# Rows for the layer's far edge: copied between the layers into pieces of their own, instead of among the stores

## The chip, the cores and the metric

One core of one Trainium2 chip runs the whole program. The metric is the device time of one execution in microseconds. The kernel before takes 3490.39 us in the median of 3 runs (3487.72 to 3494.23).

## What is computed

The input x is (8, 16, 512, 512) in fp32: 8 images of 16 channels. Two layers, each adding something to its own input:

```python
x = x + fourier_conv(gn(x))       # layer 0
x = x + mean_filter_15x15(gn(x))  # layer 1
```

`gn` normalises groups of two channels over the whole image. Layer 0 takes the real 2-D FFT of the result, does a complex 3x3 convolution with 16 to 16 channels on the spectrum, adds a bias and transforms back. Layer 1 is a 15x15 box filter of each channel with zeros outside.

```python
kh = jnp.ones((1, 1, k, 1), x.dtype) / k
kw = jnp.ones((1, 1, 1, k), x.dtype) / k
y = lax.conv_general_dilated(xr, kh, (1, 1), [(pad, pad), (0, 0)])
y = lax.conv_general_dilated(y, kw, (1, 1), [(0, 0), (pad, pad)])
```

## The kernel before

One image lies in SBUF at a time, in `img` [128 partitions, T = 64 rows, W = 512]. A partition is one channel and one of HB = 8 blocks of 64 image rows; so step t of a loop over T works on row t of all 8 blocks of all 16 channels. The program loops over the 8 images. Images 0 to 6 run in a hardware loop in which the next image is loaded; image 7 runs after it and loads nothing.

Layer 0 works without an FFT: per row, matrices that are fetched from DRAM (`bd_all`), a Hilbert transform, and wave terms; TensorE, VectorE, ScalarE and GpSimd pass the row on (`gp`, `hp`, `g32`, `xT`, `kappa`, `bias_c`, `wrap_row`, `wrap_high` are its buffers). At its end come the statistics of the new x, which give the scale and shift of layer 1's norm.

Layer 1 keeps a running sum down the rows, in PSUM:

- GpSimd's `difference(u)` (L1479) makes row u + 7 minus row u - 8 of the image.
- ScalarE's `scale_row(u)` (L944, L945) scales it with the norm.
- TensorE's `turn_step(u)` (L757) transposes it, ScalarE's `high_part` (L810) and VectorE's `low_part` (L1332) split it into two fp16 parts.
- TensorE's `box_row(u)` (L768) adds the horizontal sum of these to the running row in `p0[0]`.
- VectorE's `add_box(u)` (L1340) adds x and writes the output row into `ob`, which has NS = 3 buffers of two rows. SyncE's `store` (L371) writes buffer j % 3 to DRAM with two DMAs of 256 KB. Before an even row u = 2j, `add_box` waits until the store of pair j - 3 has landed (`stored`).

The arena is cut into 16 pieces of one row each (`piece`, 512 fp32). In layer 1 `diff` is a ring of three pieces for differences (0, 1, 11), `parts` a ring of three for the fp16 parts (2, 3, 12); pieces 14 and 15 (`head`, `tail`) are presums.

Near a block's edges the box reaches into the neighbouring blocks, which lie on other partitions. For rows 1 to 7 `difference` needs the last 7 rows of the block before; for rows 57 to 63 the first 7 rows of the block after. DMAs from SBUF to SBUF bring them, both into the same pieces 4 to 10 (`across`):

- `rows_before` (L436) runs in the gap between the layers: zeros for the first block (`no_row`), then 4 copies of 4 rows, then 4 copies of 3 rows, as the rows become final (`x1_whole`). They signal `before_in`.
- `rows_after` (L451) runs in the loop of the stores, in two parts, because the pieces have to be read for the last time first (it waits for `turned`). Part 0 (rows 0 to 3) comes behind store pair 0, part 1 (rows 4 to 6) behind store pair 2; each is five DMAs, three of them with 32 partitions, one with 16, one of zeros from DRAM. They signal `after_in`.

Who waits for `after_in`: GpSimd before difference 57, and ScalarE's `load_next` (L964), because it overwrites the rows that were copied. `load_next` issues the loads of the next image from ScalarE's queue into rows that have been stored: at u = 11, 15, 19 and so on it loads 4 rows with two DMAs of 512 KB each, 8 rows behind.

The order on each queue is that of the program text. SyncE issues everything but the loads of images 1 to 7: in layer 0 the matrices and DMA transposes, then `rows_before`, then the 32 store pairs, with `rows_after` at j = 0 and 2 and a table (`hilbert_kernel`, 256 KB, into `tail`) at j = 4.

```python
for j in range(T // 2):
    ...
    store(b, j, j % NS)
    if j in (0, 2):
        rows_after(b, j // 2)
    if j == 4:
        sp.wait_ge(turned, b * T + 1)
        sp.dma_start(tail, tab["hilbert_kernel"]).then_inc(bias_in, 16)
```

Of the kernel before, what the change touches and what calls it, by code (L numbers as in the profile page):

```python
# [32 lines left out]
F16 = mybir.dt.float16  # L33
ALU = mybir.AluOpType
ACT = mybir.ActivationFunctionType
# [126 lines left out]
def build(nc, x, w_real, w_imag, b_real, b_imag, tab, bd_dram, out):  # L162
    x_v = x.rearrange("b c (s hl t) w -> b s c hl (t w)", s=2, hl=HL)
    out_v = out.rearrange("b c (s hl t) w -> b s c hl (t w)", s=2, hl=HL)
    with ExitStack() as ctx:
        def sb(name, shape, dt=F32):
            return ctx.enter_context(nc.sbuf_tensor(name, shape, dt))
# [18 lines left out]

        diff = [piece[s] for s in (0, 1, 11)]
        parts = [piece[s].bitcast(F16).rearrange("p (l k m) -> p l k m", l=2, k=NQ) for s in (2, 3, 12)]
        head, tail = piece[14], piece[15]
        across = [piece[4 + r] for r in range(R)]  # L190
        across_all = arena[:, 4 * W:(4 + R) * W]

        def diff_row(u):
            return across[u - 1] if u <= R else diff[u % 3] if u < T - R else across[u - (T - R)]

# [22 lines left out]
        xT = [row.bitcast(F16).rearrange("p (k m) -> p k m", k=8) for row in (piece[9], xT_more[:])]  # L218
        wrap_row = sb("wrap_row", [P, W], F16)
        wrap_high = sb("wrap_high", [P, W], F16)  # L220
        block_mat = sb("block_mat", [P, 9, P])
        kappa = sb("kappa", [P, 3, T, 2])
        bias_c = sb("bias_c", [P, 2, T, 2])
        known = sb("known", [P, T, 2])
# [63 lines left out]
        scaled_row = sem("scaled_row")  # L288
        before_in, after_in = [[sem(f"{name}{s}") for s in range(2)] for name in ("before_in", "after_in")]
        turned, high_done, low_done, banded = sem("turned"), sem("high_done"), sem("low_done"), sem("banded")  # L290
# [51 lines left out]
        def _(sp):  # L342
# [92 lines left out]

            def rows_before(b):  # L436

                def shifted(first, rows, signal):
                    to, at = across_all[:, first * W:(first + rows) * W], T - R + first
                    of = img[:, at:at + rows, :].rearrange("p t w -> p (t w)")  # L440
# [4 lines left out]
                sp.dma_start(across_all[0:HP:HL], tab["no_row"]).then_inc(before_in[0], 16)  # L445
                sp.wait_ge(x1_whole, (b + 1) * T - 3)
                shifted(0, 4, before_in[0])
                sp.wait_ge(x1_whole, (b + 1) * T)
                shifted(4, 3, before_in[1])

            def rows_after(b, part):  # L451

                first, rows = ((0, CHUNK), (CHUNK, R - CHUNK))[part]
                to = across_all[:, first * W:(first + rows) * W]
                of = img[:, first:first + rows, :].rearrange("p t w -> p (t w)")
                sp.wait_ge(turned, b * T + first + rows + 1)
                for hl in range(HL - 1):
                    sp.dma_start(to[hl:P:HL], of[hl + 1:P:HL]).then_inc(after_in[part], 16)
                sp.dma_start(to[HL - 1:HP:HL], of[HP:P:HL]).then_inc(after_in[part], 16)
                sp.dma_start(to[HP + HL - 1:P:HL], tab["no_row"][:, 0:rows * W]).then_inc(after_in[part], 16)  # L460

            with sp.Fori(0, B - 1) as b:
                matrices(b)
                rows_before(b)
                for j in range(T // 2):
                    if j == T // 2 - 2:
                        sp.wait_ge(loaded_pair[LAG // 2 - 1], b * 32 + 64)
                        sp.sem_inc(stores_held, 1)
                    store(b, j, j % NS)
                    if j in (0, 2):  # L470
                        rows_after(b, j // 2)
                    if j == 4:
                        sp.wait_ge(turned, b * T + 1)
                        sp.dma_start(tail, tab["hilbert_kernel"]).then_inc(bias_in, 16)
            matrices(B - 1)
            rows_before(B - 1)
            for j in range(T // 2):
                store(B - 1, j, j % NS)
                if j in (0, 2):
                    rows_after(B - 1, j // 2)  # L480
            for s in range(NS):
# [326 lines left out]
        def _(act):  # L808
# [35 lines left out]
            def image(b, follow):  # L844
# [67 lines left out]
                act.wait_ge(v_stacked, b + 1)  # L912
                nc.scalar.activation(wrap_high[:], p0[2], ACT.Identity, scale=sc[:, 27:28]).then_inc(v_high, 1)

# [82 lines left out]
        def _(dve):  # L997
# [193 lines left out]
            def layer0(b):  # L1191
# [27 lines left out]
                def low_hilbert(n, s):  # L1219
# [6 lines left out]
                dve.wait_ge(c_made, b + 1)  # L1226
                V.tensor_copy(bias_c[:], c_tab[:, 0:2])
# [4 lines left out]
                V.scalar_tensor_tensor(wrap_row[:], p0[2], sc[:, 26:27], wrap_high[:],  # L1232
                                       ALU.mult, ALU.subtract).then_inc(v_wrap, 1)
# [139 lines left out]
        def _(pool):  # L1373
# [89 lines left out]
            def layer1(b, follow):  # L1463

                def difference(u):

                    if u <= R:
                        pool.wait_ge(before_in[0], (b + 1) * 80)
                        if u > 4:
                            pool.wait_ge(before_in[1], (b + 1) * 64)  # L1470
                        more, less = img[:, u + R, :], diff_row(u)
                    elif u < T - R:
                        if u > R + 3:
                            pool.wait_ge(turned, b * T + u - 2)
# [47 lines left out]
```

## Time and profile before

| | |
|---|---|
| runs | 3494.23, 3487.72, 3490.39 us |
| the profiled execution | 3492.99 us |
| its span, first to last instruction | 3491.0 us |
| mean granted TensorE clock | 0.980 |
| TensorE busy | 3107.4 us (89%) |
| VectorE busy | 3076.4 us (88%) |
| GpSimd busy | 2723.9 us (78%) |
| ScalarE busy | 2446.0 us (70%) |

The profile is of one execution. Times in it are microseconds from the first instruction, those that are marked so are ns. PE is TensorE, DVE VectorE, ACT ScalarE, POOL GpSimd, SP SyncE; a q behind the name is the engine's sequencer, which issues DMAs. `<-` in brackets names what ended the idle time before an instruction. An image takes some 418 us (layer 1 begins at 465.82 in image 0 and at 883.76 in image 1), of which about 120 us are rows of layer 1. Seven images have the same course, the eighth loads nothing.

### The profile page before, as it was taken

To read this page: it belongs to the slowest core of one execution; us is meant where nothing else is said; L and a number is where in the kernel's file an instruction comes from. 1 tells how busy PE (TensorE), PEld (TensorE's weight loads), DVE (VectorE), ACT (ScalarE), POOL (GpSimd) and SP (SyncE) were. 2 spreads that over 40 slices of the span, in tenths; PEclk is the share of its full clock that TensorE was granted. 3 is DMA by queue.
4 is the path that set the end of the run, shared out by engine and by line. 5 is a ranking of instruction groups with operands and counts; after the bars stand their busy time and mean duration, and the time that the engine had idled before them with its cause. 6 is when DMAs were issued, how large, how long until landed. Compare 5 with 4: busy or idle time off the path is not lost.

```text
span 3491.0 us, 110788 instructions
## 1 busy us (share of the span) xinstructions
PE 3107.4 (89%) x36064; PEld 1869.7 (54%) x36064; DVE 3076.4 (88%) x5786; ACT 2446.0 (70%) x4742; POOL 2723.9 (78%) x2231
## 2 busy tenths in 40 slices
PE   2199979999889988899899998999988999899986
PEld 1155555555555555555555555555555555555555
DVE  6789978999889988899798997999978998889987
ACT  2568865787658876588666885578865787658876
POOL 4079975899749987599776997589974998759986
PEclk9699999999999999999999999999999999999999
DMA  8656668666876659766596666966678665876655
GB/s 206 200 93 128 127 202 252 114 127 120 249 205 126 128 116 285 169 125 128 154 293 125 126 129 184 272 113 128 120 225 229 117 128 119 259 195 126 127 129 174
DMA packets 726765, 573.58 MB, mean 164 GB/s; under 512 B 592416, under 2 KB 667776, under 8 KB 712064
## 3 DMA queue, kind: packets, MB, share of 16 engines
q1 hardware_dynamic: 704000, 451.67, 56.1%
q10 hardware_dynamic: 22400, 117.46, 13.1%
q8 instruction: 178, 2.92, 0.4%
q14 instruction: 187, 1.53, 0.2%
HBM read 262.08 MB, written 148.90 MB: 118 GB/s over the span
## 4 chain that ended last, share of the span: by engine, by line
PE 59%; DVE 16%; issue 9%; POOL 5%; DMA 3%; SPq 3%; ACT 1%; ACTq 1%; DVEq 0%; POOLq 0%
PE p L626 26%; PE h_ps L536 10%; PE h_odd L536 10%; DVE ob_all L1340 6%; DVE arena L1332 4%; PE p L633 4%; POOL arena L1479 3%; PE h_ps L626 3%; DMA out<-ob_all 2%; PE p L768 2%; DVE stat L1102 2%; PE h_ps L633 1%; PE p L575 1%; SPq L371 1%; ACTq L972 1%
## 5 line engine op out<-in xcount | busy, mean ns | idle before, releaser
L626 PE MATMUL p<-arena,bd_all 64*64 64x512 f16 x16896 | 1290.7, 381 | 31.2 <-DVE ob_all L1270 22.2
L626 PEld LDWEIGHTS p<-arena,bd_all 64*64 64x64 f16 x16896 | 555.2, 105 | 374.0 <-issue 233.1
L1419 POOL TENSOR_TENSOR ob_all<-ob_all,img 128x512 f32<-128x512 f32 x512 | 664.5, 1298 | 78.5 <-DVE ob_all L1264 52.2
L1422 POOL TENSOR_TENSOR ob_all<-ob_all 128x512 f32<-128x512 f32 x512 | 654.1, 1277 | 40.1
L1479 POOL TENSOR_TENSOR arena<-img 128x512 f32<-128x512 f32 x392 | 499.0, 1275 | 177.0 <-PE h_ps L757 97.9
L1264 DVE SCALAR_TENSOR_TENSOR ob_all<-p,bias_c,cosw 128x256 f32<-128x256 f32 x1024 | 447.6, 478 | 60.1 <-PE p L626 22.6
L886 ACT ACTIVATE img<-img,half_row (+1 forms) x1024 | 487.7, 528 | 5.0 <-ACT half_row L876 0.4
L768 PE MATMUL p<-band,arena 128*128 128x135 f16 (+1 forms) x4096 | 340.3, 228 | 154.9 <-DVE ob_all L1340 149.8
L1270 DVE SCALAR_TENSOR_TENSOR ob_all<-p,bias_c,cosw 128x256 f32<-128x256 f32 x1024 | 443.2, 474 | 0.0
L1412 POOL TENSOR_TENSOR arena<-arena 128x512 f16<-128x512 f32 x256 | 308.5, 1205 | 160.5 <-ACT arena L860 160.5
L859 ACT ACTIVATE arena<-img,sc 128x512 f16 (+1 forms) x512 | 433.8, 847 | 0.0
L944 ACT ACTIVATE arena<-arena,sc 128x512 f32<-128x512 f32 x392 | 282.9, 722 | 206.6 <-POOL arena L1479 197.9
L1340 DVE SCALAR_TENSOR_TENSOR ob_all<-p,img 128x512 f32<-128x512 f32 x512 | 347.5, 679 | 88.6 <-PE p L768 55.7
L1282 DVE BATCH_NORM_STATS2 stat<-img (+1 forms) x512 | 355.7, 695 | 51.7
L768 PEld LDWEIGHTS p<-band,arena 128*128 128x128 f16 x4096 | 260.5, 99 | 259.1 <-issue 244.6
L575 PE MATMUL p<-img,bd_all 128*64 128x256 f32 x2048 | 300.1, 402 | 92.6 <-POOL bd_all L1383 66.9
L536 PE MATMUL h_ps<-hilbert,arena 128*128 128x256 f16 x3072 | 379.8, 273 | 1.2 <-DMA arena<-arena 1.2
L536 PE MATMUL h_odd<-hilbert,xT_more 128*128 128x256 f16 x3072 | 379.8, 273 | 1.0 <-DMA xT_more<-arena 0.7
L1412 POOL TENSOR_TENSOR arena<-g_more,arena 128x512 f16<-128x512 f32 x256 | 311.7, 1218 | 55.5 <-ACT g_more L860 35.5
L536 PEld LDWEIGHTS h_odd<-hilbert,xT_more 128*128 128x128 f16 x3072 | 279.8, 98 | 138.2 <-issue 91.5
L536 PEld LDWEIGHTS h_ps<-hilbert,arena 128*128 128x128 f16 x3072 | 280.2, 98 | 132.6 <-issue 98.7
L1102 DVE BATCH_NORM_STATS2 stat<-img 128x6 f32<-128x512 f32 x512 | 334.8, 680 | 0.3
(182 smaller groups left out, 5136.6 us busy)
## 6 DMA issues: line engine op xcount, KB each, us to landing
out<-ob_all SPq DMA_DIRECT2D x512, 256.0 KB, 4.5
bd_all<-bd_dram SPq DMA_DIRECT2D x512, 224.0 KB, 2.5
img<-in_x ACTq DMA_DIRECT2D x168, 512.0 KB, 6.9
img<-in_x ACTq DMA_DIRECT2D x112, 256.0 KB, 5.3
img<-in_x SPq DMA_DIRECT2D x24, 512.0 KB, 26.1
arena<-img SPq DMA_DIRECT2D x48, 256.0 KB, 3.2
arena<-img SPq DMA_DIRECT2D x48, 192.0 KB, 2.7
bd_dram<-ob_all SPq DMA_DIRECT2D x11, 768.0 KB, 3.6
```

The costliest lines, as they stand in the source:

```text
L536: m = mm(dst(a), row[:, 4 * lx + k, :], tb["hilbert16"][:, lt, k, 0:cols], start=(half == 0 and i == 0), stop=(half == 1 and i == 2))
L626: m = mm(bank[out_half * HP:(out_half + 1) * HP, :], bd[s % RB][rows, 6 * lm + (j if own else j + 1), :], part, start=opens and i3 == 0, s ...
L768: m = mm(p0[0][:, lo:hi], parts[u % 3][:, l, k, :], tb["band16"][:, lo - k * P + R:hi - k * P + R], start=(u == 0 and k == 0 and l == 0), ...
L859: nc.scalar.activation(halves(gp[s][:, 0, :]), row, ACT.Identity, bias=sc[:, 9:10], scale=sc[:, 8:9])
L886: ins = nc.scalar.activation(row, row, ACT.Identity, bias=half_row[:, s, a:a + 1])
L1264: ins = V.scalar_tensor_tensor(t1[:, a, :], p1[:, a * HALF:(a + 1) * HALF], bias_c[:, 1, t, 1 - a:2 - a], cosw[:, a, :], ALU.subtract, ALU ...
L1270: ins = V.scalar_tensor_tensor(t2[:, a, :], p2[:, a * HALF:(a + 1) * HALF], bias_c[:, 0, t, 1 - a:2 - a], sinw[:, a, :], ALU.add, ALU.mult)
L1340: V.scalar_tensor_tensor(ob[j % NS][:, u % 2, :], p0[0], 1.0 / (K * K * BOX_SCALE), img[:, u, :], ALU.mult, ALU.add).then_inc(row_out, 1)
L1412: G.tensor_tensor(gp[s][:, 1, :], g32[s % 2], gp[s][:, 0, :], ALU.subtract).then_inc(g_split, 1)
L1419: G.tensor_tensor(q, term_row[s % 2][0], parity(img[:, t, :]), ALU.add).then_inc(first_added, 1)
L1422: G.tensor_tensor(q, q, term_row[s % 2][1], ALU.add).then_inc(q_done, 1)
L1479: G.tensor_tensor(diff_row(u), more, less, ALU.subtract).then_inc(moved, 1)
```

## The change

The rows of the block before go to pieces 0 to 6, those of the block after to pieces 7 to 13. They no longer share pieces, so the rows of the block after need not wait for a reader. All copies are issued in the gap between the layers (`rows_across`): the three DMAs of 32 partitions with 7 rows each stand between the two batches of rows of the block before, the DMA of 16 partitions and the one of zeros behind both. The store loop keeps the stores and the table. `rows_after` with its two parts is gone; `after_in` is one semaphore.

The rings that lay in these pieces go to buffers of layer 0 that layer 1 doesn't use: `diff` to `g32_more`, `xT_more` and the memory of `kappa` and `bias_c` (now one tensor, `biases`), `parts` to two stretches of `bd_all` and to `wrap_row` with `wrap_high` (now one tensor, `wrap_rows`). The rings keep three buffers.

```diff
-        diff = [piece[s] for s in (0, 1, 11)]
-        parts = [piece[s].bitcast(F16).rearrange("p (l k m) -> p l k m", l=2, k=NQ) for s in (2, 3, 12)]
         head, tail = piece[14], piece[15]
-        across = [piece[4 + r] for r in range(R)]
-        across_all = arena[:, 4 * W:(4 + R) * W]
+        rows_of_before, rows_of_after = arena[:, 0:R * W], arena[:, R * W:2 * R * W]
 
         def diff_row(u):
-            return across[u - 1] if u <= R else diff[u % 3] if u < T - R else across[u - (T - R)]
+            return piece[u - 1] if u <= R else diff[u % 3] if u < T - R else piece[R + u - (T - R)]
...
+        flat16 = bd_all[:].rearrange("p s r -> p (s r)")
+        diff = [g32_more[:], xT_more[:], biases[:, 0:W]]
+        parts = [row.rearrange("p (l k m) -> p l k m", l=2, k=NQ)
+                 for row in (flat16[:, 0:2 * W], flat16[:, 4 * W:6 * W], wrap_rows[:])]
...
                 sp.wait_ge(x1_whole, (b + 1) * T - 3)
                 shifted(0, 4, before_in[0])
+                to, of = rows_of_after, rows_of(0, R)
+                for hl in range(HL - 1):
+                    sp.dma_start(to[hl:P:HL], of[hl + 1:P:HL]).then_inc(after_in, 16)
                 sp.wait_ge(x1_whole, (b + 1) * T)
                 shifted(4, 3, before_in[1])
-
-            def rows_after(b, part):
-
-                first, rows = ((0, CHUNK), (CHUNK, R - CHUNK))[part]
-                to = across_all[:, first * W:(first + rows) * W]
-                of = img[:, first:first + rows, :].rearrange("p t w -> p (t w)")
-                sp.wait_ge(turned, b * T + first + rows + 1)
-                for hl in range(HL - 1):
-                    sp.dma_start(to[hl:P:HL], of[hl + 1:P:HL]).then_inc(after_in[part], 16)
-                sp.dma_start(to[HL - 1:HP:HL], of[HP:P:HL]).then_inc(after_in[part], 16)
-                sp.dma_start(to[HP + HL - 1:P:HL], tab["no_row"][:, 0:rows * W]).then_inc(after_in[part], 16)
+                sp.dma_start(to[HL - 1:HP:HL], of[HP:P:HL]).then_inc(after_in, 16)
+                sp.dma_start(to[HP + HL - 1:P:HL], tab["no_row"]).then_inc(after_in, 16)
...
                     store(b, j, j % NS)
-                    if j in (0, 2):
-                        rows_after(b, j // 2)
                     if j == 4:
                         sp.wait_ge(turned, b * T + 1)
                         sp.dma_start(tail, tab["hilbert_kernel"]).then_inc(bias_in, 16)
...
                     if t < R:
-                        act.wait_ge(after_in[t // CHUNK], (b + 1) * (16 * COPIES))
+                        act.wait_ge(after_in, (b + 1) * (16 * COPIES))
...
-                        pool.wait_ge(after_in[0 if u - (T - R) < CHUNK else 1], (b + 1) * (16 * COPIES))
+                        pool.wait_ge(after_in, (b + 1) * (16 * COPIES))
```

SyncE in the gap between the layers, before: a row is a line of the kernel, the destination and source of the DMA, partitions x elements, how many of them, and the semaphore that is waited for ahead of it; 2048 elements are 4 rows of the image, 1536 are 3, 3584 are 7.

```order
L445 DMA arena<-tab_no_row 16x3584 [waits p0_ready]
L442 DMA arena<-img 32x2048 [waits x1_whole]
L442 DMA arena<-img 32x2048 x2
L443 DMA arena<-img 16x2048
L442 DMA arena<-img 32x1536 [waits x1_whole]
L442 DMA arena<-img 32x1536 x2
L443 DMA arena<-img 16x1536
L371 ISA [waits row_out]
```

And now:

```order
L449 DMA arena<-tab_no_row 16x3584 [waits p0_ready]
L446 DMA arena<-img 32x2048 [waits x1_whole]
L446 DMA arena<-img 32x2048 x2
L447 DMA arena<-img 16x2048
L454 DMA arena<-img 32x3584 x3
L446 DMA arena<-img 32x1536 [waits x1_whole]
L446 DMA arena<-img 32x1536 x2
L447 DMA arena<-img 16x1536
L457 DMA arena<-img 16x3584
L458 DMA arena<-tab_no_row 16x3584
```

The three DMAs of L454 stand ahead of the wait for the last rows, two more behind the second batch.

SyncE at the stores around part 1 of `rows_after`, before: store pair 2 (four rows of L371, the first of which waits for the rows), the five copies, store pair 3.

```order
L371 ISA [waits row_out]
L371 DMA out<-ob_all 16x4x1024
L371 ISA
L371 DMA out<-ob_all 16x4x1024
L458 DMA arena<-img 32x1536 [waits turned]
L458 DMA arena<-img 32x1536 x2
L459 DMA arena<-img 16x1536
L460 DMA arena<-tab_no_row 16x1536
L371 ISA [waits row_out]
L371 DMA out<-ob_all 16x4x1024
L371 ISA
L371 DMA out<-ob_all 16x4x1024
```

And now, pairs 2 and 3:

```order
L373 ISA [waits row_out]
L373 DMA out<-ob_all 16x4x1024
L373 ISA
L373 DMA out<-ob_all 16x4x1024
L373 ISA [waits row_out]
L373 DMA out<-ob_all 16x4x1024
L373 ISA
L373 DMA out<-ob_all 16x4x1024
```

The copies are gone from between the pairs, and likewise those between pairs 0 and 1: each pair waits for its rows alone.

## Rows read from the trace of the kernel before

**Rows 1.** The page: the span; the group of add_box (columns: title of part 5).
```profile
span 3491.0 us, 110788 instructions
...
L1340 DVE SCALAR_TENSOR_TENSOR ob_all<-p,img 128x512 f32<-128x512 f32 x512 | 347.5, 679 | 88.6 <-PE p L768 55.7
```

**Rows 2.** Waits of the whole span (who <- whom: us in total, times, longest).
```profile
DVE ob_all L1340 <- PE p L768: 55.7, 168, 1.1
...
DVE ob_all L1340 <- DMA out<-ob_all: 32.7, 11, 4.9
```

**Rows 3.** Timeline, VectorE, image 0 (start us, us, ..., [idle <-releaser]).
```profile
465.82 0.68 DVE L1340 SCALAR_TENSOR_TENSOR ob_all<-p,img 128x512 f32<-128x512 f32 x1
...
482.92 0.69 DVE L1340 SCALAR_TENSOR_TENSOR ob_all<-p,img 128x512 f32<-128x512 f32 x1 [0.24 <-PE p L768]
...
489.07 0.69 DVE L1340 SCALAR_TENSOR_TENSOR ob_all<-p,img 128x512 f32<-128x512 f32 x1 [4.86 <-DMA out<-ob_all]
...
491.04 0.69 DVE L1340 SCALAR_TENSOR_TENSOR ob_all<-p,img 128x512 f32<-128x512 f32 x1 [0.68 <-PE p L768]
...
494.97 0.69 DVE L1340 SCALAR_TENSOR_TENSOR ob_all<-p,img 128x512 f32<-128x512 f32 x1 [0.24 <-PE p L768]
```

**Rows 4.** Timeline, VectorE, image 6, add_box of rows 0 and 15.
```profile
2972.67 0.68 DVE L1340 SCALAR_TENSOR_TENSOR ob_all<-p,img 128x512 f32<-128x512 f32 x1
...
3001.23 0.69 DVE L1340 SCALAR_TENSOR_TENSOR ob_all<-p,img 128x512 f32<-128x512 f32 x1 [0.67 <-PE p L768]
```

**Rows 5.** Timeline, VectorE, image 7 (no loads), rows 0 and 15.
```profile
3388.11 0.68 DVE L1340 SCALAR_TENSOR_TENSOR ob_all<-p,img 128x512 f32<-128x512 f32 x1
...
3411.44 0.69 DVE L1340 SCALAR_TENSOR_TENSOR ob_all<-p,img 128x512 f32<-128x512 f32 x1 [0.24 <-PE p L768]
```

**Rows 6.** Timeline, the queue of SyncE, image 0 (columns as in Rows 3).
```profile
449.21 0.59 SPq L443 DMA_DIRECT2D arena<-img  x1
453.97 1.74 SPq L442 DMA_DIRECT2D arena<-img  x3
...
473.09 2.87 SPq L371 DMA_DIRECT2D out<-ob_all  x4
476.00 2.49 SPq L458 DMA_DIRECT2D arena<-img  x3
...
479.17 0.59 SPq L460 DMA_DIRECT2D arena<-tab_no_row  x1
479.95 3.09 SPq L371 DMA_DIRECT2D out<-ob_all  x4
```

**Rows 7.** Timeline, the queue of ScalarE, image 0.
```profile
478.93 0.70 ACTq L972 DMA_DIRECT2D img<-in_x  x1
...
485.39 1.28 ACTq L972 DMA_DIRECT2D img<-in_x  x2
...
505.00 0.55 ACTq L972 DMA_DIRECT2D img<-in_x  x1
```

**Rows 8.** Chain of work, image 0 (start us, us, what).
```profile
480.75 8.30 DMA out<-ob_all
```

**Rows 9.** DMA issues at 477 to 478.9: KB each, median us to landing.
```profile
arena<-img SPq DMA_DIRECT2D x3, 192.0 KB, 3.0
```

**Rows 10.** DMA issues at 506.5 to 507.8, the same columns.
```profile
out<-ob_all SPq DMA_DIRECT2D x2, 256.0 KB, 6.6
```

**Rows 11.** Windows (line above the rows: columns), image 0.
```profile
core 0: us, PE busy (x) PEld busy (x) DVE busy (x) ACT busy (x) POOL busy (x), PEclk, DMA share, GB/s
...
470.00:481.00 11.00, 7.75 (x89) 6.28 (x87) 9.14 (x15) 7.95 (x14) 8.29 (x8) 1.00 0.92 299
481.00:485.00 4.00, 2.90 (x33) 2.24 (x30) 2.67 (x5) 3.30 (x7) 3.18 (x4) 1.00 1.03 240
486.00:489.00 3.00, 0.00 (x0) 0.00 (x0) 0.00 (x0) 0.72 (x1) 0.77 (x2) 0.54 1.03 404
...
500.00:560.00 60.00, 59.50 (x533) 36.91 (x532) 59.67 (x101) 39.87 (x67) 47.12 (x43) 1.00 0.99 288
```

**Rows 12.** DMA queues at 481.9 to 485.2: packets, MB, share of 16 engines.
```profile
q10 hardware_dynamic: 93, 0.62, 80.3%
q1 hardware_dynamic: 35, 0.11, 13.8%
```

**Rows 13.** DMA issues at 485.38 to 486.5 (columns as in Rows 9).
```profile
out<-ob_all SPq DMA_DIRECT2D x1, 256.0 KB, 10.6
```

**Rows 14.** Timeline, GpSimd, image 0, the first differences.
```profile
460.12 8.66 POOL L1479 TENSOR_TENSOR arena<-img,arena 128x512 f32<-128x512 f32 x7 [4.75 <-DVE arena L1345]
```

More of the change, by code:

```diff
@@ L218, in build @@
         xT = [row.bitcast(F16).rearrange("p (k m) -> p k m", k=8) for row in (piece[9], xT_more[:])]
-        wrap_row = sb("wrap_row", [P, W], F16)
-        wrap_high = sb("wrap_high", [P, W], F16)
+        wrap_rows = sb("wrap_rows", [P, 2 * W], F16)
+        wrap_row, wrap_high = wrap_rows[:, 0:W], wrap_rows[:, W:2 * W]
         block_mat = sb("block_mat", [P, 9, P])
-        kappa = sb("kappa", [P, 3, T, 2])
-        bias_c = sb("bias_c", [P, 2, T, 2])
+        biases = sb("biases", [P, 5 * 2 * T])
+        kappa = biases[:, 0:6 * T].rearrange("p (f t a) -> p f t a", f=3, a=2)
+        bias_c = biases[:, 6 * T:10 * T].rearrange("p (f t a) -> p f t a", f=2, a=2)
+        flat16 = bd_all[:].rearrange("p s r -> p (s r)")
+        diff = [g32_more[:], xT_more[:], biases[:, 0:W]]
+        parts = [row.rearrange("p (l k m) -> p l k m", l=2, k=NQ)
+                 for row in (flat16[:, 0:2 * W], flat16[:, 4 * W:6 * W], wrap_rows[:])]
         known = sb("known", [P, T, 2])
@@ L288, in build @@
         scaled_row = sem("scaled_row")
-        before_in, after_in = [[sem(f"{name}{s}") for s in range(2)] for name in ("before_in", "after_in")]
+        before_in, after_in = [sem(f"before_in{s}") for s in range(2)], sem("after_in")
         turned, high_done, low_done, banded = sem("turned"), sem("high_done"), sem("low_done"), sem("banded")
@@ L434, in matrices, with rows_across, rows_of @@
                 fetch(T - 1, (T - 1) % RB)
-            def rows_before(b):
+            def rows_across(b):
+                def rows_of(first, rows):
+                    return img[:, first:first + rows, :].rearrange("p t w -> p (t w)")
                 def shifted(first, rows, signal):
-                    to, at = across_all[:, first * W:(first + rows) * W], T - R + first
-                    of = img[:, at:at + rows, :].rearrange("p t w -> p (t w)")
+                    to, of = rows_of_before[:, first * W:(first + rows) * W], rows_of(T - R + first, rows)
                     for hl in range(HL - 1):
@@ L444, in rows_before @@
                 sp.wait_ge(p0_ready, (b + 1) * T + PRIMED)
-                sp.dma_start(across_all[0:HP:HL], tab["no_row"]).then_inc(before_in[0], 16)
+                sp.dma_start(rows_of_before[0:HP:HL], tab["no_row"]).then_inc(before_in[0], 16)
                 sp.wait_ge(x1_whole, (b + 1) * T - 3)
                 shifted(0, 4, before_in[0])
+                to, of = rows_of_after, rows_of(0, R)
+                for hl in range(HL - 1):
+                    sp.dma_start(to[hl:P:HL], of[hl + 1:P:HL]).then_inc(after_in, 16)
                 sp.wait_ge(x1_whole, (b + 1) * T)
                 shifted(4, 3, before_in[1])
-            def rows_after(b, part):
-                first, rows = ((0, CHUNK), (CHUNK, R - CHUNK))[part]
-                to = across_all[:, first * W:(first + rows) * W]
-                of = img[:, first:first + rows, :].rearrange("p t w -> p (t w)")
-                sp.wait_ge(turned, b * T + first + rows + 1)
-                for hl in range(HL - 1):
-                    sp.dma_start(to[hl:P:HL], of[hl + 1:P:HL]).then_inc(after_in[part], 16)
-                sp.dma_start(to[HL - 1:HP:HL], of[HP:P:HL]).then_inc(after_in[part], 16)
-                sp.dma_start(to[HP + HL - 1:P:HL], tab["no_row"][:, 0:rows * W]).then_inc(after_in[part], 16)
+                sp.dma_start(to[HL - 1:HP:HL], of[HP:P:HL]).then_inc(after_in, 16)
+                sp.dma_start(to[HP + HL - 1:P:HL], tab["no_row"]).then_inc(after_in, 16)
             with sp.Fori(0, B - 1) as b:
                 matrices(b)
-                rows_before(b)
+                rows_across(b)
                 for j in range(T // 2):
@@ L475, in _ @@
             matrices(B - 1)
-            rows_before(B - 1)
+            rows_across(B - 1)
             for j in range(T // 2):
                 store(B - 1, j, j % NS)
-                if j in (0, 2):
-                    rows_after(B - 1, j // 2)
             for s in range(NS):
@@ L912, in image @@
                 act.wait_ge(v_stacked, b + 1)
-                nc.scalar.activation(wrap_high[:], p0[2], ACT.Identity, scale=sc[:, 27:28]).then_inc(v_high, 1)
+                nc.scalar.activation(wrap_high, p0[2], ACT.Identity, scale=sc[:, 27:28]).then_inc(v_high, 1)
                 def slot(i, s, first):
@@ L1226, in layer0 @@
                 dve.wait_ge(c_made, b + 1)
-                V.tensor_copy(bias_c[:], c_tab[:, 0:2])
+                V.tensor_copy(bias_c, c_tab[:, 0:2])
                 lk(V.scalar_tensor_tensor(known[:], c_tab[:, 2], unscale, parity_mean, ALU.mult, ALU.add))
@@ L1231, in layer0 @@
                 dve.wait_ge(v_high, b + 1)
-                V.scalar_tensor_tensor(wrap_row[:], p0[2], sc[:, 26:27], wrap_high[:],
+                V.scalar_tensor_tensor(wrap_row, p0[2], sc[:, 26:27], wrap_high,
                                        ALU.mult, ALU.subtract).then_inc(v_wrap, 1)
```

## The prediction, as it stood before the change was run

> **What bounds the kernel now.** The page comes first, for the size of things: a span of 3491.0 us in an execution of 3492.99 us, and `add_box` (L1340), VectorE's last step of every row of layer 1 [rows 1]. The waits of the whole span say what this step waits for. Most of it is TensorE in small pieces of at most 1.1 us; but 32.7 us are eleven waits for a store of `ob_all` to land, the longest 4.9 us [rows 2]. Few and long: that is one place, not a rate.
>
> The timeline of VectorE shows the place. In image 0 `add_box` of row 0 starts at 465.82 and that of row 11 at 482.92, one row each 1.55 us. Row 12 starts at 489.07 after 4.86 us idle, "<-DMA out<-ob_all"; rows 13 and 15 still have 0.68 and 0.24 us of TensorE before them, and row 15 starts at 494.97 [rows 3]. So row 15 is 29.15 us behind row 0. In image 6 it is 28.56 us [rows 4]; in image 7, where no next image is loaded, 23.33 us [rows 5]. The disturbed images lose 5.8 and 5.2 us against the last one: I take **5.5 us in each of 7 images**, 38.7 us in all. (4.7 us of it is the wait itself, 32.7 / 7; the rest is TensorE coming back.)
>
> Why does row 12 wait? Store pair j takes rows 2j and 2j+1 out of one of three `ob` buffers, so row 12 needs pair 3 (rows 6 and 7) landed. Row 7 was ready at 477.4 (row 11's start less four periods, plus 0.69). But SyncE's queue shows L458, L459 and L460 from 476.00 to 479.76, the five copies of `rows_after` part 1, and pair 3 only behind them, at 479.95 [rows 6]. Meanwhile ScalarE's queue issued the first two loads of the next image, 512 KB each, at 478.93 and 479.79 [rows 7]. So the copies pushed the pair from 1.5 us ahead of the loads to 1.0 us behind them. Its second half, issued at 480.75, took 8.30 us and ended the wait at 489.05 [rows 8].
>
> **The change part by part.**
> *Removed.* SyncE issues ten copies fewer among the stores of each image. Part 0 sat where the queue had slack: nothing waits for pairs 0 to 2, I price it at nothing. Without part 1, pair 3 is issued at 477.4 and 478.2. Copies issued at 477 to 478.9, just as far ahead of the loads, landed in 3.0 us [rows 9]: the pair lands at about 481.5, and row 12 is due at 484.5. The wait at row 12 goes, with what follows it: at most −5.5 us an image.
>
> *What is late next.* Pair 4 (rows 8, 9) is ready at 480.5, and its second half is issued at 481.3, 1.6 us behind a load's issue. The nearest pair in that position (506.55, load at 505.00 [rows 7]) took 6.6 us in the median [rows 10]: landed at 488, row 14 is due at 487.6. I price it at 0 to 0.5 us, inside the next figure.
> Pair 5 (rows 10, 11) is ready at 483.6, behind the 256 KB copy of `hilbert_kernel` that stays where it was (j == 4). Row 16 is due at 491.0. The next two loads were issued at 485.39 [rows 7], a place that TensorE and ScalarE set before row 12's wait, so it stays. What must the 16 DMA engines move by then? Loads alone moved at 240 GB/s (481 to 485), stores after them at 404 GB/s (486 to 489), both with the engines full [rows 11]. From 481.0: two loads (1.05 MB) 4.4 us, pair 4 1.3 us, the table 1.1 us at the rate of a load, pair 5 1.3 us: 489.1, about 490 with the landing. But the second two loads join 2 us after their issue, at 487.4, with 1.7 us of this left. How are the engines shared then? At 481.9 to 485.2, with pairs waiting, ScalarE's queue (q10) held 80.3% of them and SyncE's (q1) 13.8% [rows 12]. With a fifth for the stores the pair lands at about 494.5 and row 16 waits 3.5 us; with half, at 491.8 and it waits 0.8 us. The worst pair of this stretch took 10.6 us from 485.29 [rows 13]; from 484.4 that would be 495.0, a wait of 4.0 us. The best case is none. I take 2.2 us, midway between the two shares, and 0.3 us for TensorE after it: **+2.5 us**.
>
> The Trainium skill (DMA: Bandwidth & Descriptors, Queues, rings and completion order) states that each engine goes round robin between the queue rows that have work, packet by packet. By that rule the wait at row 16 would be the 0.8 us of equal shares or less, and the sum 33 us or more, as in the second rival. This case's trace doesn't show equal turns: 13.8% against 80.3% in the stretch above [rows 12], so I keep the middle.
>
> *Added in the gap.* SyncE issues three copies of 448 KB (7 rows, 32 partitions) between the two batches of rows from the block before, and two of 224 KB behind. Issuing costs 0.6 us each, 449.85 to 451.8, and SyncE waits until 453.97 anyway [rows 6], so the second batch (L442, then L443) isn't issued later. But its 0.67 MB is behind 1.34 MB more. At the 299 GB/s of mixed copies and stores [rows 11] the three take 4.5 us from 452.6 and the batch 2.2 us more: landed at 460.3 instead of 458. Its first reader is GpSimd's difference of row 5. The first difference starts at 460.12, seven take 8.66 us [rows 14]: the fifth starts at 465.1. The cover is 4.8 us; if it were gone, every us of delay would be one on GpSimd, ahead of ScalarE and TensorE. Price: nothing. The last two copies are wanted by ScalarE's first load, 18 us later: nothing.
>
> *Moved rings.* `diff` and `parts` lie elsewhere, with three buffers as before, the same waits and the same instructions. No engine gets a longer operand. ScalarE's and GpSimd's waits on `after_in` become one wait that is long over. Nothing.
>
> *Behind row 16.* From 500 to 560 VectorE is busy 59.67 of 60 us, so rows come at its own pace, but the DMA engines are at 0.99 too [rows 11]. Copies of 1.8 MB leave this stretch, so a shift of rows 16 to 63 is kept; image 7 has no wait and gains nothing.
>
> **Sum:** (5.5 − 2.5) × 7 = 21 us off 3492.99, 3472 us. The profiled execution is 2.6 us above the median of the runs (3490.39), so I predict **3469 us**. 0.2%, some 7 us, is about what a measurement of this kernel can tell from no change.
>
> **The rivals.**
> 1. *Forecast: the wait shrinks and moves to row 16*, 0.8 to 3.5 us: 12 to 33 us off (the upper wait with 0.3 us of TensorE, the lower with none), 3457 to 3478. For it: the shares of 80.3% and 13.8% [rows 12]. Chance 0.55.
> 2. *It is gone:* pair 5 gets enough of the engines, because pair 3 and the last copies no longer queue in the way of the first loads: 38.7 us off, 3452. For it: the sum of work ends at 490, a microsecond before it is due. Against it: the table ahead of the pair. Chance 0.28.
> 3. *The change doesn't do what it says:* the loads, not the copies, hold up the stores, and the waits at rows 12 to 16 add up to what was there: 3490. For it: the 10.6 us of a pair with no copy ahead of it. Chance 0.11.
> 4. *The DMA engines become the bound, slower:* the wait at row 12 was a pause in which they caught up. Without it rows 16 to 56 carry a backlog, with store packets and load packets mixed all the time. Four rows are 2.1 MB; at the 288 GB/s of 500 to 560 they take 7.3 us, while VectorE needs 7.1 (101 instructions in 60 us, three a row [rows 11]). At 264 GB/s, midway to the 240 of loads alone, they take 7.95: 0.8 us on each of ten groups, 8 against the 5.5 us saved, 2.5 × 7 = 18 us more, 3508. It decides below 274 GB/s, where ten groups lose 5.5 us. Against it: the bytes from row 16 on are the same as before, and they fitted. Chance 0.06.
>
> **Range.** The full gain less a margin of 2 us gives 3450. The worst single pair (4.0 us, and 0.8 us of TensorE, whose granted clock was 0.54 at 486 to 489 [rows 11], near its lower level of 1.2 GHz, after it had stood idle in the wait) leaves 0.7 us × 7 = 5 us, 3485; the two shares end at 3478. I set the upper end at 3484, which leaves out rivals 3 and 4, 0.17. Faster: 0.83, the first two; same: 0.11; slower: 0.06.
>
> **What would show it.** Right: no "<-DMA out<-ob_all" before row 12 in images 0 to 6; pair 3 issued at once when row 7 is ready, landing in 3 to 4 us; a wait of about 2 us before row 16, its pair's second half landing close to the second loads; the copies of L454 and the batch behind them landed before GpSimd's fifth difference; image 7 unchanged. Wrong: a wait before row 5 of the differences; a wait that stays at row 12 with pair 3 issued early; waits at rows 14 or 30 and later that weren't there; or rows 16 to 56 slower than 1.8 us each, which would say that the DMA engines are the bound.

## The result, and the profile after

| | before | changed |
|---|---|---|
| median of the runs | 3490.39 us (5 runs, 3487.72 to 3494.23) | 3470.51 us (5 runs, 3466.16 to 3473.83) |
| ratio | | 0.9938, 95% interval 0.9926 to 0.9949 |
| the profiled execution | 3492.99 us | 3473.83 us |

Faster by 0.62%, 19.9 us by the medians, 19.2 us between the two profiled executions. The range of the prediction holds it, and the time is 1.5 us off the predicted one.

The page of the changed kernel: the span, and `add_box`, which is L1334 now [rows 1].

```profile
span 3471.8 us, 110748 instructions
...
L1334 DVE SCALAR_TENSOR_TENSOR ob_all<-p,img 128x512 f32<-128x512 f32 x512 | 348.2, 680 | 65.9 <-PE p L762 48.0
```

Waits of the whole span (who <- whom: us in total, times, longest), against [rows 2]:

```profile
DVE ob_all L1334 <- PE p L762: 48.0, 171, 1.2
...
DVE ob_all L1334 <- DMA out<-ob_all: 17.5, 20, 1.8
```

32.7 us in eleven waits have become 17.5 us in twenty, the longest 1.8 us. The waits are fewer microseconds, and they are spread.

The timeline of VectorE in image 0, rows 0, 11, 12, 14, 15, 16 and 18 of `add_box` [rows 3]:

```profile
466.87 0.68 DVE L1334 SCALAR_TENSOR_TENSOR ob_all<-p,img 128x512 f32<-128x512 f32 x1
...
483.97 0.69 DVE L1334 SCALAR_TENSOR_TENSOR ob_all<-p,img 128x512 f32<-128x512 f32 x1 [0.23 <-PE p L762]
...
485.57 0.69 DVE L1334 SCALAR_TENSOR_TENSOR ob_all<-p,img 128x512 f32<-128x512 f32 x1 [0.31 <-PE p L762]
...
489.71 0.69 DVE L1334 SCALAR_TENSOR_TENSOR ob_all<-p,img 128x512 f32<-128x512 f32 x1 [1.33 <-DMA out<-ob_all]
...
491.23 0.69 DVE L1334 SCALAR_TENSOR_TENSOR ob_all<-p,img 128x512 f32<-128x512 f32 x1 [0.23 <-PE p L762]
...
493.04 0.67 DVE L1334 SCALAR_TENSOR_TENSOR ob_all<-p,img 128x512 f32<-128x512 f32 x1
...
496.97 0.69 DVE L1334 SCALAR_TENSOR_TENSOR ob_all<-p,img 128x512 f32<-128x512 f32 x1 [0.27 <-DMA out<-ob_all]
```

Row 12 follows row 11 by 1.60 us, without a wait for a store. Row 14 waits 1.33 us, row 18 0.27 us. Row 15 stands 24.36 us behind row 0, where it stood 29.15.

The timeline of SyncE's queue in image 0 [rows 6]:

```profile
450.89 2.79 SPq L454 DMA_DIRECT2D arena<-img  x3
455.02 1.74 SPq L446 DMA_DIRECT2D arena<-img  x3
456.80 0.59 SPq L447 DMA_DIRECT2D arena<-img  x1
457.44 0.59 SPq L457 DMA_DIRECT2D arena<-img  x1
458.07 0.59 SPq L458 DMA_DIRECT2D arena<-tab_no_row  x1
469.26 13.72 SPq L373 DMA_DIRECT2D out<-ob_all  x10
483.09 0.60 SPq L470 DMA_DIRECT2D arena<-tab_hilbert_kernel  x1
484.83 4.39 SPq L373 DMA_DIRECT2D out<-ob_all  x4
```

The timeline of ScalarE's queue there [rows 7]:

```profile
479.99 0.69 ACTq L966 DMA_DIRECT2D img<-in_x  x1
...
486.45 1.55 ACTq L966 DMA_DIRECT2D img<-in_x  x2
```

The stores from 469.26 on are one run of ten DMAs, five pairs. DMA issues in three windows, 478.5 to 479.9, 481.5 to 482.9 and 484.5 to 486 (KB each, median us to landing), which are pairs 3, 4 and 5:

```profile
out<-ob_all SPq DMA_DIRECT2D x2, 256.0 KB, 3.0
...
out<-ob_all SPq DMA_DIRECT2D x2, 256.0 KB, 6.8
...
out<-ob_all SPq DMA_DIRECT2D x2, 256.0 KB, 6.2
```

Pair 3 is issued ahead of the loads (479.99) and lands in 3.0 us, pair 4 behind them in 6.8 us, pair 5 in 6.2 us. In the gap, the instructions of line L446 from 454.5 to 457, the second batch:

```profile
DMA to landing us min/median/max: 2.4/2.5/2.5
```

And the timeline of GpSimd's first differences [rows 14]:

```profile
461.17 8.66 POOL L1473 TENSOR_TENSOR arena<-img,arena 128x512 f32<-128x512 f32 x7 [4.76 <-DVE arena L1339]
```

No idle time inside the seven differences: the batch in the gap (issued by 457.4, landed in 2.5 us) was there 6 us before the fifth began at 466.1.

The table below says where the time went. Each number is the start of `add_box` of that row behind row 0 of its image, from the timeline, in the mean of images 0 to 6. The experiments that follow stand in the same table. "Stores" is the total of "DVE ob_all <- DMA out<-ob_all" in the waits.

| kernel | row 12 | row 14 | row 16 | row 24 | row 56 | row 63 | stores, us | median, us |
|---|---|---|---|---|---|---|---|---|
| before | 22.83 | 27.21 | 30.80 | 45.11 | 102.76 | 118.58 | 32.7 | 3490.39 |
| changed | 18.69 | 22.68 | 26.43 | 41.33 | 99.37 | 115.60 | 17.5 | 3470.51 |
| e1 copies back among the stores | 22.75 | 27.06 | 30.53 | 44.87 | 102.55 | 118.32 | 32.3 | 3491.18 |
| e2 small copies, load held too | 19.73 | 23.96 | 27.51 | 42.35 | 100.00 | 115.88 | 12.6 | 3470.07 |
| e3 before, without part 1 | 18.69 | 22.90 | 27.33 | 42.67 | 100.95 | 116.65 | 22.7 | 3463.47 |
| e4 table behind pair 0 | 18.69 | 22.67 | 26.00 | 40.85 | 98.67 | 114.66 | 13.1 | 3461.36 |
| e5 small copies, load not held | 21.87 | 26.10 | 29.53 | 43.84 | 101.83 | 117.75 | 27.1 | 3487.54 |
| e6 loads one row later | 18.79 | 23.23 | 26.82 | 41.62 | 98.98 | 115.16 | 11.9 | 3471.19 |
| e7 four store buffers | 18.69 | 21.81 | 25.15 | 39.45 | 96.97 | 112.71 | none | 3457.05 |
| e8 before, four buffers | 18.69 | 22.81 | 26.27 | 40.78 | 98.28 | 114.24 | 10.1 | 3464.82 |
| e9 four buffers, table first | 18.69 | 21.81 | 25.14 | 39.44 | 96.95 | 112.97 | none | 3452.99 |
| e10 before, part 1 behind pair 3 | 18.69 | 25.57 | 30.22 | 45.19 | 102.90 | 118.71 | 30.6 | 3494.76 |

The change saves 4.1 us an image at row 12, 4.4 at row 16, 3.8 at row 24, 3.4 at row 56 and 3.0 at row 63. 3.0 × 7 is 20.9 us (unrounded), the whole result of 19 to 20 us: row 0 of image 0 stands 1.05 us later in this execution (466.87 against 465.82), which takes the rest back. Image 7 stays at 98.13 us for row 63, as before. The rows are those of one execution of each kernel, the medians those of all its runs.

### The profile page after: what moved, and what is told of

The parts are those of the page before. It is cut to its first block, busy times and chain, and to the rows that moved or that the text cites. A ratio compares the mean times of both kernels' runs of the same rounds, so it can differ in the third digit from the quotient of the medians.

```text
span 3471.8 us, 110748 instructions
## 1 busy us (share of the span) xinstructions
PE 3104.5 (89%) x36064; PEld 1865.1 (54%) x36064; DVE 3079.8 (89%) x5786; ACT 2444.9 (70%) x4742; POOL 2726.1 (79%) x2231
## 3 DMA queue, kind: packets, MB, share of 16 engines
q10 hardware_dynamic: 22400, 117.46, 13.1%
## 4 chain that ended last, share of the span: by engine, by line
PE 61%; DVE 13%; issue 11%; POOL 7%; DMA 4%; SPq 2%; ACT 2%; ACTq 1%; DVEq 0%; POOLq 0%
PE p L620 26%; PE h_ps L530 10%; PE h_odd L530 10%; DVE ob_all L1334 5%; PE p L627 4%; PE p L762 3%; PE h_ps L620 3%; DMA out<-ob_all 2%; PE p L569 2%; DVE bd_all L1326 2%; POOL xT_more L1473 1%; POOL biases L1473 1%; POOL g_more L1473 1%; PE h_ps L627 1%; DVE stat L1096 1%
## 5 line engine op out<-in xcount | busy, mean ns | idle before, releaser
L1258 DVE SCALAR_TENSOR_TENSOR ob_all<-p,biases,cosw 128x256 f32<-128x256 f32 x1024 | 447.9, 479 | 59.3 <-PE p L620 21.7
L1264 DVE SCALAR_TENSOR_TENSOR ob_all<-p,biases,cosw 128x256 f32<-128x256 f32 x1024 | 443.5, 474 | 0.0
L1334 DVE SCALAR_TENSOR_TENSOR ob_all<-p,img 128x512 f32<-128x512 f32 x512 | 348.2, 680 | 65.9 <-PE p L762 48.0
L762 PE MATMUL p<-band,bd_all 128*128 128x135 f16 (+1 forms) x2752 | 227.0, 227 | 94.8 <-DVE ob_all L1334 90.1
L627 PE MATMUL p<-wrap_rows,bd_all 64*64 64x512 f16 x1536 | 302.6, 381 | 0.7
L1273 DVE SCALAR_TENSOR_TENSOR img<-p,sc,ob_all 128x512 f32 (+1 forms) x384 | 285.3, 743 | 17.3 <-POOL ob_all L1416 17.3
L861 ACT ACTIVATE arena<-h_odd 128x512 f16<-128x512 f32 x256 | 152.9, 597 | 193.9 <-PE h_odd L530 193.9
```

Of the source, the lines that this page charges most:

```text
L627: m = mm(p0[s % RB][out_half * HP:(out_half + 1) * HP, :], wrap_mat[s % RB][half * HP:(half + 1) * HP, out_half * HP:(out_half + 1) * HP], ...
L1258: ins = V.scalar_tensor_tensor(t1[:, a, :], p1[:, a * HALF:(a + 1) * HALF], bias_c[:, 1, t, 1 - a:2 - a], cosw[:, a, :], ALU.subtract, ALU ...
L1264: ins = V.scalar_tensor_tensor(t2[:, a, :], p2[:, a * HALF:(a + 1) * HALF], bias_c[:, 0, t, 1 - a:2 - a], sinw[:, a, :], ALU.add, ALU.mult)
L1334: V.scalar_tensor_tensor(ob[j % NS][:, u % 2, :], p0[0], 1.0 / (K * K * BOX_SCALE), img[:, u, :], ALU.mult, ALU.add).then_inc(row_out, 1)
```

## The experiments

Each was run beside the kernel before on the same chip: medians of 3487.79 us for e1 to e4, 3491.44 for e5 to e8, 3490.96 for e9 and e10. The theory: part 1's copies delayed the issue of store pair 3 until it stood behind ScalarE's loads. Rivals: the bytes of the copies, the new places of the rings, part 0.

**e1.** The changed kernel, copies back behind pairs 0 and 2, but into their own pieces.

```diff
-                for hl in range(HL - 1):
-                    sp.dma_start(to[hl:P:HL], of[hl + 1:P:HL]).then_inc(after_in, 16)
...
                     store(b, j, j % NS)
+                    if j in (0, 2):
+                        rows_after(b, j // 2)
```

> The changed kernel with its pieces and rings kept, but the copies of the block after put back among the stores (behind pairs 0 and 2). If the place of the copies in SyncE's queue is the cause: 3490 us (3485 to 3495), a wait of 4 to 5 us before row 12 in images 0 to 6 as in the kernel before. Rival, the other buffers for the rings bring the gain: 3470.

Measured: 3491.18 us, ratio 1.001 (1.000 to 1.002). Its timeline, row 12 of image 0:

```profile
487.13 0.69 DVE L1343 SCALAR_TENSOR_TENSOR ob_all<-p,img 128x512 f32<-128x512 f32 x1 [4.78 <-DMA out<-ob_all]
```

The wait is back with 4.78 us and the whole gain is gone. The rings in other buffers bring nothing; the place of the copies is all of it.

The kernel before holds a second control. In image 7 the same five copies stand between pairs 2 and 3, but no load is issued. Pair 3, issued from 3402.07 on, lands in 3.3 us, and no row waits for a store. DMA issues at 3402.05 to 3403.2:

```profile
out<-ob_all SPq DMA_DIRECT2D x2, 256.0 KB, 3.3
```

So the copies alone, bytes and issuing time both, don't make the wait. It takes the loads.

**e2.** Issuing time without bytes: five copies of 8 KB behind pair 2.

```diff
+            def small_copies(b):
+                sp.wait_ge(after_in, b * 160 + 80)
+                for k in range(5):
+                    sp.dma_start(rows_of_after[0:P:HL, k * 64:(k + 1) * 64],
+                                 img[1:P:HL, 0, k * 64:(k + 1) * 64]).then_inc(after_in, 16)
```

> The changed kernel with five copies of 8 KB each behind store pair 2: the issuing time of part 1 (some 3 us) without its 0.8 MB. If what counts is that the pair of rows 6 and 7 is issued behind the loads instead of ahead of them: most of the gain gone, the wait at row 12 back with 3 to 5 us, 3482 to 3490. Rival, the bytes of the copies are what delays it: within 4 us of 3470.

Measured: 3470.07 us, ratio 0.9954 (0.9936 to 0.9971). By its expectation the rival wins. But the timeline of the two queues (SyncE's rows, then ScalarE's) says that it didn't ask the question:

```profile
476.52 3.19 SPq L463 DMA_DIRECT2D arena<-img  x5
479.89 2.97 SPq L373 DMA_DIRECT2D out<-ob_all  x4
...
481.06 1.58 ACTq L975 DMA_DIRECT2D img<-in_x  x2
```

The small copies count on `after_in` too, so ScalarE waited for them before its first load: it came at 481.06, still behind pair 3 (479.89 and 480.69). Pair 3 was 1.6 us later, counted from row 0, and kept its place ahead of the load. That most of the gain stayed says something after all: it is not the time of issue by itself that matters. But the second half, 0.4 us ahead of the load, was already near the edge: it landed in 3.3 to 3.7 us in four images and in 5.4 to 5.7 us in three (images 1, 2 and 4). Row 12 stands 1.0 us later than in the changed kernel (19.73); I put this down to ScalarE's own wait, which isn't shown apart.

**e5** mends this: the same copies to a tensor of their own (`spare`), with a semaphore that the first loads don't wait for (that of rows 16 to 19 does).

```diff
+                    sp.dma_start(spare[0:P:HL, k * 64:(k + 1) * 64],
+                                 img[1:P:HL, 20, k * 64:(k + 1) * 64]).then_inc(small_in, 16)
```

> As the small copies before (five of 8 KB behind pair 2, in the changed kernel), but with a semaphore of their own, so that ScalarE's first load isn't held back for them: pair 3 is now issued behind the loads, as in the kernel before, with no bytes ahead of it. If the order of issue of pair 3 and the loads is what counts: row 12 waits 2.5 to 4.5 us again, row 16 stands at 29 to 30.5 us from row 0 (before 30.8, changed 26.4), 3480 to 3490. Rival, it takes the 0.8 MB: row 12 waits under 1.5 us, within 6 us of 3470.

Measured: 3487.54 us, ratio 0.9989 (0.9980 to 0.9999). The timeline of SyncE's queue, of ScalarE's, and row 12 on VectorE:

```profile
476.97 3.28 SPq L464 DMA_DIRECT2D spare<-img  x5
480.43 2.21 SPq L375 DMA_DIRECT2D out<-ob_all  x3
...
480.17 0.72 ACTq L978 DMA_DIRECT2D img<-in_x  x1
...
489.72 0.69 DVE L1346 SCALAR_TENSOR_TENSOR ob_all<-p,img 128x512 f32<-128x512 f32 x1 [4.28 <-DMA out<-ob_all]
```

Pair 3 at 480.43, a quarter of a microsecond behind the load at 480.17, and 40 KB of copies in place of 0.8 MB: row 12 waits 4.28 us, and 3.2 to 3.5 us in the other six images. Row 16 stands 3.1 us later than in the changed kernel (29.53 against 26.43) of the 4.1 us that the real copies cost (e1, 30.53). The last microsecond isn't one of bytes in the main: from row 0 on, in the mean of seven images, the second half of pair 3 was issued at 14.18 us here and at 14.88 in e1, 0.7 us later, and took 7.7 us to land here and 7.8 there. So 40 KB or 0.8 MB ahead of it makes some 0.2 us of the landing; the order of issue, and how far behind the load, makes nearly all of it.

**e3.** The kernel before, without part 1.

```diff
+                if part == 1:
+                    sp.sem_inc(after_in[1], 16 * COPIES)
+                    return
```

> The kernel before without the five copies of part 1 (rows 4 to 6 of the block after are not brought; the last rows of each block use what lies there). Part 0 stays among the stores. If part 1 alone makes the wait: 3470 (3464 to 3474), row 12 without a wait, row 14 with about 1 us. Rival, part 0 takes its share too: 3476 to 3484.

Measured: 3463.47 us (4 runs, 3460.68 to 3475.72), ratio 0.9931 (0.9914 to 0.9949). The profile is that of the 3475.72. Row 12 has no wait in any image, row 14 waits:

```profile
488.35 0.69 DVE L1343 SCALAR_TENSOR_TENSOR ob_all<-p,img 128x512 f32<-128x512 f32 x1 [1.53 <-DMA out<-ob_all]
```

Part 1 alone made the wait at row 12. By the medians part 0, still among the stores, costs nothing that the interval can tell; the time is half a microsecond under the 3464 to 3474 expected. The rows don't settle it: in the profiled execution, 12 us above the median, row 16 has a wait of 1.1 to 1.7 us in five of seven images, and row 63 stands 1.05 us behind the changed kernel's (116.65 against 115.60). Whether part 0 has a small price behind row 14 stays open.

**e10.** The kernel before, part 1 behind pair 3.

```diff
-                    if j in (0, 2):
+                    if j in (0, 3):
```

> The kernel before with the five copies of part 1 behind store pair 3 instead of pair 2. Pair 3 is then issued ahead of the loads, and row 12 doesn't wait. The copies now push pair 4 (rows 8, 9) back to some 482.4, behind the loads and the copies: it lands at 489.5 to 490.5 and row 14 waits 2 to 3 us; ScalarE's second load waits for the copies too, 1 to 3 us more. 3474 to 3488: there is no free place for them among these stores. Rival, only row 12's pair is that sensitive: 3466 to 3472, as with the changed kernel.

Measured: 3494.76 us, ratio 1.0008 (0.9998 to 1.0018). The timeline of SyncE's queue, and row 14 on VectorE:

```profile
476.05 1.27 SPq L371 DMA_DIRECT2D out<-ob_all  x2
477.37 2.01 SPq L458 DMA_DIRECT2D arena<-img  x3
...
481.12 1.37 SPq L371 DMA_DIRECT2D out<-ob_all  x2
...
489.98 0.69 DVE L1340 SCALAR_TENSOR_TENSOR ob_all<-p,img 128x512 f32<-128x512 f32 x1 [4.15 <-DMA out<-ob_all]
```

The time lies outside what either theory gave. Row 12 is cured, as said; row 14 waits 4.15 us, more than the 2 to 3 expected, since pair 4, now at 481.12, stands behind the loads (477.44) and the copies both. ScalarE's second pair of loads came 25.0 us behind row 0 in place of 19.6, once the copies had landed at 24.5. The wait was moved whole. Neither of the two places tried, behind pair 2 and behind pair 3, is free.

**e4.** The changed kernel, table behind pair 0.

```diff
-                    if j == 4:
+                    if j == 0:
                         sp.wait_ge(turned, b * T + 1)
                         sp.dma_start(tail, tab["hilbert_kernel"]).then_inc(bias_in, 16)
```

> The changed kernel with the 256 KB table issued behind store pair 0 instead of pair 4. If the rest of the waits at rows 14 to 22 come from all that the engines must move in 481 to 495: the wait at row 14 stays (about 1 us, its pair is ahead of the table), those at rows 16 to 22 shrink, 0.5 to 1.2 us an image, 3462 to 3467. Rival, the engines have slack from row 24 on anyway and the end of the loads sets the end of the layer: within 3 us of 3470.

Measured: 3461.36 us, ratio 0.9928 (0.9907 to 0.9949). Row 14 is where it was (22.67), rows 16 to 63 are 0.4 to 0.9 us earlier, 6.6 us over seven images. The interval overlaps that of the change (0.9926 to 0.9949), so the runs alone don't tell the two apart; the row positions of one execution each do point the way that was expected.

**e6.** The changed kernel, loads one row later.

```diff
-                        k = u // CHUNK - 2
-                        if u % CHUNK == CHUNK - 1 and 0 <= k < NCH - LAG // CHUNK:
+                        k = u // CHUNK - 3
+                        if u % CHUNK == 0 and 0 <= k < NCH - LAG // CHUNK:
```

> The changed kernel with each load of four rows issued one row later (u = 12, 16, ... instead of 11, 15, ...), so that the store pair that now follows a load by 1.6 us is issued at about the same time as it. If a pair is late only by what the loads ahead of it hold: no wait at row 14, few anywhere, row 16 at 25 to 26 us, 3458 to 3466. Rival, the engines' total work sets rows 16 to 24 in any order: within 3 us of 3470. Second rival, the loads come too late for the counting of rows from row 16 on: slower than 3475.

Measured: 3471.19 us, ratio 0.9947 (0.9931 to 0.9964), as the first rival said. The wait at row 14 didn't go; the row stands 0.5 us later (23.23). DMA issues in three windows show the halves of pair 4: in image 0 the first (issued 480.69) and the second (481.42; the loads at 480.56 and 481.43), then in image 1 the first (893.07, its load at 892.92):

```profile
out<-ob_all SPq DMA_DIRECT2D x1, 256.0 KB, 2.9
...
out<-ob_all SPq DMA_DIRECT2D x1, 256.0 KB, 6.9
...
out<-ob_all SPq DMA_DIRECT2D x1, 256.0 KB, 5.8
```

In image 0 the half issued 0.1 us behind a load landed in 2.9 us, as if no load were there. That was an exception: in the other six images the same half, 0.1 us behind its load as well, took 5.5 to 5.9 us. The second half, 0.9 us behind the load, took 6.9 us in image 0 and 7.5 to 8.5 us in the others. A pair is as late as its second half, so issuing it at about the same time as the load brings nothing.

**e7.** The changed kernel with NS = 4.

```diff
-NS = 3
+NS = 4
```

> The changed kernel with NS = 4 buffers of two rows for the stores. If landing of the pair of six rows back is the only thing that layer 1 waits for beyond VectorE's pace: no wait for a store, row 16 at 25.0 us, row 56 at 96.6 us (72 times 1.79 less), 3445 to 3456. Rival, the engines become the bound of rows 16 to 56: waits remain, over 3460.

Measured: 3457.05 us, ratio 0.9898 (0.9881 to 0.9914), a microsecond above the range of the theory and under the rival's 3460. No wait for a store is left in the trace. Rows 16 to 56 take 71.8 us (25.15 to 96.97), VectorE's pace: the DMA engines aren't the bound there. The rows gain 2.9 us an image over the changed kernel at row 63, 20.2 us over seven images, the profiled execution only 15.4 us. From row 63 to row 0 of the next image it takes 0.8 us longer (299.74 against 298.97 us in the mean); why is open.

**e8.** The kernel before with NS = 4.

```diff
-NS = 3
+NS = 4
```

> The kernel before with NS = 4. Row 12 then needs pair 2, row 14 needs pair 3 (landed at 489.05 where it is due at 487.6): a wait of 1 to 2 us in place of 4.7. If the copies cost through the landing of pair 3 alone, they cost 1 to 2 us an image here: 3455 to 3466, and 7 to 14 us over the changed kernel with four buffers. Rival, they cost their share of the engines however deep the buffers are: 20 us over it.

Measured: 3464.82 us, ratio 0.9929 (0.9912 to 0.9945). Waits of its span:

```profile
DVE ob_all L1340 <- DMA out<-ob_all: 10.1, 10, 2.2
```

Row 14 now needs the late pair 3 and stands 1.0 us behind e7, row 63 1.5 us. With the deeper ring the misplaced copies cost 7.8 us by the medians, 1.5 × 7 = 10.7 by the rows, in place of 20. And a fourth buffer alone does at least as well as the change: the ratios are 0.9929 and 0.9938, with intervals that overlap, and row 63 stands 1.4 us ahead of the changed kernel's (114.24 against 115.60).

**e9.** Four buffers and the table behind pair 0, the changed kernel otherwise.

> The changed kernel with NS = 4 and the table behind pair 0. If no store is waited for with four buffers, the table costs nothing there and its move gives nothing: 3457 within 4 us, no wait for a store. Rival, the table still takes engine time that the loads need, so that their end comes earlier without it: 3448 to 3453.

Measured: 3452.99 us (4 runs, 3447.29 to 3454.51), ratio 0.9884 (0.9867 to 0.9900). No wait for a store, rows as in e7 (row 56 at 96.95, row 63 at 112.97). The rows of layer 1 gain nothing over e7, as the first theory said; but the median is 4.1 us under e7's, just outside the 4 us that it allowed and inside the rival's 3448 to 3453. The intervals of the two ratios overlap, so the time doesn't decide between the two, and whether the table has a price with four buffers stays open. It is the version with the lowest median of the study: 1.2% under the kernel before, 17.5 us under the changed one by the medians, which were taken in different sessions.

## Why the prediction was right, and where it was not

*Where the time was lost.* Right. The wait at row 12 was the copies' doing, through the queue (e1, e5), part 1's alone (e3), and it takes the loads as well (image 7).

*Removed: 5.5 us an image.* Right in kind, size good: at row 15 the kernels with four buffers, which have no wait at all, stand at 23.3 us like image 7. Pair 3 was issued at 478.60, as soon as row 7 was ready, and landed in 3.0 us, the figure taken from [rows 9].

*Pair 4, "0 to 0.5 us, inside the next figure".* Mis-sized. The nearest pair of [rows 10] had a median of 6.6 us for two halves; the ring waits for the second half, and that took 7.25 us in image 0. The chain of work there (start us, us, what):

```profile
482.44 7.25 DMA out<-ob_all
```

Row 14 is 0.9 us behind e7 in the mean (22.68 against 21.81). It waits in all seven images, 8.2 of the 17.5 us; the longest single wait, 1.75 us, is at row 50 of image 2. The forecast had the wait move to row 16: it moved to row 14.

*Pair 5: +2.5 us at row 16.* Mis-sized the other way. Row 16 stands 1.28 us behind e7 (26.43 against 25.15), most of it row 14's. Only three of seven images have a wait of their own there (image 2, 1.5 us, the longest). The term of 2 us between a load's issue and its joining had no row behind it: in the changed kernel the first packet of the first load comes some 1.5 us after its issue in each image. The 240 GB/s of "loads alone" held 0.11 MB of stores in 0.96 MB. Shares of the DMA queues, the first window (482.9 to 486.2) with pair 4 waiting beside the first loads, the second (488.6 to 492.9) with the table and pairs 5 and 6 beside the second loads:

```profile
q10 hardware_dynamic: 112, 0.73, 82.2%
q1 hardware_dynamic: 18, 0.07, 6.0%
...
q10 hardware_dynamic: 112, 0.80, 69.3%
q1 hardware_dynamic: 183, 0.52, 32.9%
```

In the first the stores got 6.0%, less than the fifth; in the second 32.9%, between the fifth and the half. Pair 5's second half landed in 7.3 us, at 492.9, between my two ends. What made it cheap is that row 14's wait had already put row 16's due time a microsecond back. Waits for landings don't add: each is a time on the clock, and a wait ahead of it is taken off.

The Trainium skill's rule (DMA: Bandwidth & Descriptors, Queues, rings and completion order: round robin between the queue rows, packet by packet) holds in neither window if it is read as equal time. By the packets that the profile counts (112 of q10 to 18 of q1, then 112 to 183), if they are the page's packets, the first isn't turn by turn either. Still, the rule's price for row 16, 0.8 us or less, was nearer to the 1.28 us that row 16 lost than my 2.5.

*Behind row 16, "a shift of rows 16 to 63 is kept".* Wrong. The saving is 4.4 us at row 16 and 3.0 us at row 63. With rows 16 to 24 at 14.90 us against 14.31 before, I read this as the backlog that the pause at row 12 used to clear, the fourth rival's mechanism at a small size. What the trace shows are waits of 0.3 to 1.8 us at rows 18, 22, 30, 34, 46, 50 and 58, other rows in each image: 7.2 us in all behind row 16, where the kernel before has 1.6 us at rows 30, 50 and 54. That difference, 0.8 us an image, is over half of the 1.4 us lost there. Waits at rows 14 or 30 and later were among the prediction's own signs of being wrong. Its decisive point (5.5 us lost) was never near, and e7 shows that a landing that nobody waits for costs layer 1 nothing: the DMA engines keep up with VectorE.

So the sum was right to 1.5 us partly by luck: 3.0 us an image came out as predicted, but as 4.4 − 1.4, where the prediction had 3.0 at row 16 and nothing lost after.

*The gap: nothing.* Right, with more to spare. The copies moved faster than I took: the second batch landed 2.5 us after issue, at about 459, not 460.3 (in an execution that stands 1 us later), 6 us before its reader. L454 was issued by 453.7, and SyncE waited for the last rows until 455.02 anyway.

*Rings and image 7: nothing.* Right (e1; image 7 at 98.13 us for row 63 in both).

*Not tried:* whether the copies in the gap would be free if they were larger, and which part of a DMA engine decides the shares between the two queues.

## What to carry to other kernels

Where two queues feed the same DMA engines, read in which order their transfers are issued, not only how long each takes: here a store of 256 KB that the queue's own side copies pushed behind a bulk load of another queue took 8 us to land in place of 3, and the pair behind it was next in line. Move side copies to a stretch in which the engines are idle, then look for the next wait, since what was a pause for the engines is gone too. And before trimming such a queue, try one more buffer in the ring that waits: here it was worth at least as much (e8, 26.6 us under its runs of before) as the change (19.9 us).

## What the runs showed that was not expected

The side of a load has an edge less than a microsecond wide. Store halves issued 0.7 us or more ahead of the first load of 512 KB landed in 2.9 to 3.1 us in all seven images of the changed kernel, and those issued 0.3 us behind it in 5.3 to 6.0 us (e5). Between the two it goes either way: 0.4 us ahead, 3.3 to 3.7 us in four images and 5.4 to 5.7 us in three (e2); 0.1 us behind, 2.9 us in one image and 5.5 to 5.9 us in six (e6). One image's landing tells little there.

And shares between the two queues aren't fixed: 6.0% to 82.2% in one window and 32.9% to 69.3% in the next, in the same image.
